# Mamba stage: convolution taps loaded by overlapping transfers, the scan's last columns kept by ScalarE, the convolution carry set earlier

## The chip, the cores and the metric

One NeuronCore of a Trainium2 chip runs the whole program. The metric is the device time of one execution in microseconds. The kernel before takes 4458.61 us (median of three runs, 4454.52 to 4467.43). The engines are TensorE (PE in the rows), VectorE (DVE), ScalarE (ACT), GpSimd (POOL) and SyncE (SP), which here only issues transfers. 16 DMA engines carry the transfers.

## The reference, cut to what matters

The network works on 16 images of 24 channels and 56 x 56 pixels. Four mixing layers (window attention, Mamba, four-way scan, row LSTM) alternate with quantised feed-forward layers. The change touches the Mamba layer alone. For a batch of images it computes:

```
x, gate   = 3x3 depthwise convolution of in_proj(normed)       # "taps": nine shifted copies of normed
xm, z     = in_proj2(x);  xm = silu(conv1d over 3 pixels(xm))   # needs the last 2 pixels of the part before: the carry
dt, B, C  = projections of xm;  dt = softplus(dt)
h[d,n]    = exp(dt*A[d,n]) * h[d,n] + dt*xm*B[n]                # a scan over the 3136 pixels, 48 channels x 16 states
y         = sum_n h[d,n]*C[n] + xm*D;  y = y * silu(z);  out = out_proj(...) * silu(gate)
```

## The kernel before, in words

The Mamba stage is `mamba_phase`, code written out for each engine in its own order, with semaphores between them. The image is cut into 7 stages of 8 rows (448 pixels). A *pair* (item `m`) is two images in one stage: 8 pairs in a stage, 56 in all. The scan works in *steps* `t` (336, 48 in a stage): two of the 16 states for 8 channels of all 16 images, so 128 lanes by 448 pixels. Eight steps are a pass (8 channels, all states), six passes a stage.

Each engine runs one loop over `j` from -11 to 66, in six slots `k`, with `t = 6j + k`. In iteration `j` the front work of pair `j+11` is done (project the taps, SiLU), the inner work of pair `j+10`, the rest of pair `j+9`, six scan steps, and the output work of pair `j-10`. So there are eleven iterations without scan steps, 45 with front work and scan steps, 11 with scan steps but no front work, and a tail.

- SP issues all transfers in order on one queue. In an iteration: the taps of pair `j+12` (`load_taps`, L1113, slot 0, two buffers), the store of B and C of pair `j+9` (L1143, `dram_bc<-mam_bcs`, 2 x 32 rows of 448), two stores each of dt, xm and z (L1121, 6 x 8 rows of 448 each), the store of the gate (L1138, `dram_gs<-mam_gs`, 128 rows); from pair 0 on also loads of dt and xm for a pass (`mam_ft`), of z (`mam_zy`) and the store of y; from `j` = 9 on loads of y and the gate (`mam_yt`, `mam_gt`) and stores of the result. In each stage four times two loads of B and C into 128 lanes (L1167, `mam_bs`, `mam_cs`, 896 KB each), the last of them behind the taps of an iteration.
- Taps: for each image of a pair nine transfers of 24 channels x 464 pixels (1856 bytes a row), one for each tap of the 3x3 window.
- DVE: two `drive` multiplications (L1500) and two scans (L1513) a step; every second step `save` (L1523) copies the last column of four rows of `h` into `kept`, where the next stage's scans start. `h` holds four steps.
- ACT: two `decay` exponentials a step (L1417), two steps ahead; then, in slots 3 to 5, SiLU and the logarithms of the front and inner work.
- POOL: `weigh` (L1570) each step; `carry` (L1578, L1580), which copies the two last pixels between parts of an image and stands in slot 1 of the iteration in which PE convolves, behind `series`; `clip` and `series`.
- PE: projections, `convolve` (L1257, waits for `carried`), and the sum over states (L1301).

Of the kernel before, what the change touches and what calls it, by code (L numbers as in the profile page):

```python
# [13 lines left out]
ACT = mybir.ActivationFunctionType  # L14
# [4 lines left out]
C = 24  # L19
# [8 lines left out]
PAD = SIDE + 2  # L28
PADDED = PAD * PAD + 4
# [5 lines left out]
def reached(eng, sem, value):  # L35

    if isinstance(value, int) and value <= 0:
        return
    eng.wait_ge(sem, value)  # L39
# [928 lines left out]
STATES = 16  # L968
# [17 lines left out]
def mamba_phase(nc, w, x, normed, mixed):  # L986
# [4 lines left out]
    with ExitStack() as ctx:  # L991
# [90 lines left out]
        def item(i):  # L1082
            return i if 0 <= i < ITEMS else None
# [7 lines left out]
        with nc.Block() as block:  # L1091
            @block.sync
            def _(sp):
# [11 lines left out]
                def load_taps(m):  # L1105
                    s, q = divmod(m, DUOS)
                    reached(sp, front_b, m - 1)
                    for i in range(2):
                        for tap in range(TAPS_5 + TAPS_4):
                            at = (8 * s + tap // 3) * PAD + tap % 3  # L1110
                            tile, row = ((taps_5, tap) if tap < TAPS_5
                                         else (taps_4, tap - TAPS_5))
                            sp.dma_start(tile[m % 2][i][C * row:C * row + C, :],  # L1113
                                         normed[2 * q + i, :, at:at + TAP_N]
                                         ).then_inc(taps_in[m % 2], 16)

                def keep_rows(dram, tile, m, sem):
# [115 lines left out]
            def _(pe):  # L1233
# [7 lines left out]
                def project(m, i):  # L1241

                    if i == 0:
                        pe.wait_ge(taps_in[m % 2], 288 * (m // 2 + 1))
                    ps = (ps_a, ps_b)[i]
                    for part, (tile, weights) in enumerate(((taps_5, win_5), (taps_4, win_4))):
                        rows = tile[m % 2][i][:].rearrange("c (r q) -> c r q", q=PAD)
                        mm = pe.matmul(ps[:, 0:MT], weights[:, i, :], rows[:, :, 0:SIDE],  # L1248
                                       start=(part == 0), stop=(part == 1))
                    mm.then_inc((front_a, front_b)[i], 1)  # L1250
# [84 lines left out]
            def _(act):  # L1335
# [74 lines left out]
                def decay(t):  # L1410
# [4 lines left out]
                    for i in range(2):  # L1415
                        at = p % DB * STATES + 2 * pair + i
                        act.activation(a[t % 3][:, i, :], ft[p % 2][:, 0, :], ACT.Exp,  # L1417
                                       scale=a_neg[:, at:at + 1]).then_inc(decays, 1)

                for j in range(FIRST, LAST):  # L1420
                    front, inner, r = item(j + LEAD), item(j + LEAD - 1), item(j - LAG)
                    for k in range(6):
                        t = 6 * j + k + 2
                        if 0 <= t < STEPS:
                            decay(t)
                        if k == 2 and item(j - LAG - 1) is not None:
                            take_result(j - LAG - 1)
                        if k == 3 and (front is not None or inner is not None):
                            load_silu(nc)
                            if front is not None:  # L1430
                                gate_image(front, 0)
                                gate_image(front, 1)
                            if inner is not None:
                                activate_inner(inner)
                                activate_z(inner)
                            load_exp_and_ln(nc)
                        if k == 4 and inner is not None:
                            step_logs(inner)
                        if k == 5 and inner is not None:
                            copy_bc(inner)  # L1440
                        if k == 5 and r is not None:
                            copy_inner(r)
                        if k == 5 and inner is not None:
                            quadratic(inner)

            @block.vector
            def _(dve):
# [55 lines left out]
                def scan(t, i):  # L1503
                    p, pair = divmod(t, 8)
                    n = 2 * t + i
                    at = p % DB * STATES + 2 * pair + i
                    dve.wait_ge(driven, n + 1)
                    if i == 0:
                        reached(dve, weighed, t - 3)
                        if t % 2 == 0:  # L1510
                            reached(dve, saved, (t - 48) // 2 + 1)
                    dve.wait_ge(decays, n + 1)
                    dve.tensor_tensor_scan(h[:, n % 8, :], a[t % 3][:, i, :], dbx[:, i, 0:MT],  # L1513
                                           kept[:, at:at + 1], ALU.mult, ALU.add
                                           ).then_inc(scanned, 1)

                def save(t):

                    p, pair = divmod(t, 8)
                    at = p % DB * STATES + 2 * pair - 2  # L1520
                    row = (2 * t - 2) % 8
                    dve.wait_ge(scanned, 2 * t + 2)
                    dve.tensor_copy(kept[:, at:at + 4], h[:, row:row + 4, MT - 1]  # L1523
                                    ).then_inc(saved, 1)

                def times_z(p):
                    dve.wait_ge(accumulated, 8 * (p + 1))
# [12 lines left out]
                for j in range(FIRST, LAST):  # L1540
                    previous = item(j + LEAD - 2)
                    for k in range(6):
                        t = 6 * j + k
                        if 0 <= t < STEPS:
                            if t % 8 == 0:
                                make_u(t // 8)
                            drive(t, 0)
                            drive(t, 1)
                        if t % 2 == 0 and 0 < t <= STEPS:
                            save(t - 1)  # L1550
                        if t % 8 == 3 and 0 <= t // 8 - 1 < PASSES:
                            times_z(t // 8 - 1)
                        if k == 2 and previous is not None:
                            step_size(previous)
                        if 0 <= t < STEPS:
                            scan(t, 0)
                            scan(t, 1)

            @block.gpsimd
            def _(pool):  # L1560
# [36 lines left out]
                    pool.tensor_tensor(yi[:], yi[:], gt[r % 2][:], ALU.mult).then_inc(gated, 1)  # L1597

                for j in range(FIRST, LAST):
                    inner, previous = item(j + LEAD - 1), item(j + LEAD - 2)  # L1600
                    for k in range(6):
                        t = 6 * j + k
                        if 0 <= t < STEPS:
                            weigh(t)
                        if k == 0 and previous is not None:
                            series(previous)
                        if k == 0 and item(j - LAG - 1) is not None:
                            times_gate(j - LAG - 1)
                        if k == 1 and inner is not None:
                            carry(inner)  # L1610
                        if k == 4 and inner is not None:
                            clip(inner)

# [639 lines left out]
```

## Time and profile before

| | us |
|---|---|
| median of three runs | 4458.61 |
| the profiled execution's own time | 4458.26 |
| its span | 4456.6 |
| Mamba stage within it, from its first load (1022.70) to the next layer's first load (2656.51) | 1634 |

Busy time in the whole span: PE 3640.5 us (82%), DVE 2888.3 (65%), ACT 2692.4 (60%), POOL 1600.1 (36%). A time in the trace counts from the span's start. The busy share of DMA is a mean over the 16 DMA engines: 0.13 is two of sixteen engines busy. For DMA a packet is one row of data or one small write of a semaphore.

### The profile page before, as it was taken

What the parts mean: (1) busy time and instruction counts of PE and PEld (TensorE: products, weight loads), DVE (VectorE), ACT (ScalarE), POOL (GpSimd) and SP (SyncE); (2) the same over time, 40 slices, a digit from 0 to 9 for tenths busy, and PEclk for the clock granted to TensorE, in tenths of its full rate; (3) what the DMA queues carried; (4) which work ended last, traced back from release to release, by engine and by line L of the source; (5) the groups of instructions that cost most, each with busy time, mean ns of one, the idle gap of its engine ahead of it and who ended that gap; (6) DMA issues with size and microseconds to landing.
All of it is one profiled execution on the core that took longest, in us unless ns stands there. A gap on an engine that the chain in (4) does not pass through costs nothing. (4 is left out here: it accounts for less than half of the span.)

```text
span 4456.6 us, 73149 instructions
## 1 busy us (share of the span) xinstructions
PE 3640.5 (82%) x20680; PEld 2121.9 (48%) x20680; DVE 2888.3 (65%) x4570; ACT 2692.4 (60%) x4664; POOL 1600.1 (36%) x1447
## 2 busy tenths in 40 slices
PE   4899999785677888888876658689999786799956
PEld 2788888442233333333332214344444332799932
DVE  2666666671289989898999937566666665111146
ACT  4555555695666767676765328677777576233346
POOL 0333333101366767676766630045555400000000
PEclk9999999897889989999999979899999988899979
DMA  3000000123536364646544122100000022100012
GB/s 92 19 15 14 14 14 14 35 57 99 152 102 162 116 177 116 172 125 166 152 135 129 52 69 50 39 16 15 15 15 15 9 53 71 34 11 11 11 44 53
DMA packets 203144, 296.59 MB, mean 67 GB/s; under 512 B 68686, under 2 KB 188670, under 8 KB 202242
## 3 DMA queue, kind: packets, MB, share of 16 engines
q1 hardware_dynamic: 193798, 285.57, 24.4%
q10 hardware_dynamic: 9216, 9.65, 0.9%
q8 instruction: 37, 0.61, 0.1%
q14 instruction: 93, 0.76, 0.1%
HBM read 193.01 MB, written 102.03 MB: 66 GB/s over the span
## 5 line engine op out<-in xcount | busy, mean ns | idle before, releaser
L1570 POOL TENSOR_TENSOR mam_hc<-mam_h,mam_cs 128x896 f32<-128x896 f32 x336 | 712.5, 2126 | 333.4 <-DVE mam_h L1513 317.3
L1301 PE MATMUL mam_ps_y<-mam_hc,mam_ident 128*128 128x448 f32 x1344 | 628.4, 595 | 211.0 <-POOL mam_hc L1570 211.0
L1513 DVE TENSOR_TENSOR_SCAN mam_h<-mam_a,mam_kept,mam_dbx 128x448 f32<-128x448 f32 x672 | 729.3, 1123 | 1.2 <-ACT mam_a L1417 1.2
L1417 ACT ACTIVATE mam_a<-mam_ft,mam_a_neg 128x448 f32<-128x448 f32 x672 | 402.1, 656 | 242.4 <-DVE mam_h L1513 241.8
L1944 POOL TENSOR_TENSOR scan_ch<-scan_h,scan_cs 128x392 f32<-128x392 f32 x256 | 344.2, 1360 | 560.8 <-DVE scan_h L1910 560.8
L1301 PEld LDWEIGHTS mam_ps_y<-mam_hc,mam_ident 128*128 128x128 f32 x1344 | 261.3, 204 | 550.0 <-POOL mam_hc L1570 330.7
L1500 DVE TENSOR_TENSOR mam_dbx<-mam_ps_u,mam_bs 128x448 f32<-128x448 f32 x672 | 381.8, 611 | 92.5 <-DMA mam_cs<-dram_bc 91.1
L756 POOL TENSOR_TENSOR att_prob<-att_prob,att_share 128x588 f32<-128x588 f32 x128 | 151.9, 1186 | 452.1 <-DVE att_share L941 452.1
L1910 DVE TENSOR_TENSOR_SCAN scan_h<-scan_turned_in,scan_start 128x392 f32<-128x392 f32 x192 | 256.6, 1356 | 25.6 <-ACT scan_turned_in L1829 24.2
L1784 PE MATMUL scan_ps_merged<-scan_ch,scan_w_merge 128*128 128x392 f32 x512 | 230.6, 532 | 47.8 <-POOL scan_ch L1944 46.0
L2034 PE MATMUL lstm_ps<-lstm_hs,lstm_w_h 128*128 (+1 forms) x1344 | 264.9, 352 | 0.0
L2034 PEld LDWEIGHTS lstm_ps<-lstm_hs,lstm_w_h 128*128 128x128 f32 x1344 | 253.1, 188 | 3.0
L2084 DVE TENSOR_TENSOR lstm_kept<-lstm_gates,lstm_cell 128x224 f32<-128x224 f32 x56 | 22.0, 392 | 347.3 <-ACT lstm_gates L2055 347.3
L408 PE MATMUL f_xc_ff<-all_x,f_centre 128*128 (+1 forms) x256 | 128.3, 585 | 145.2 <-DVE all_x L298 145.2
L2025 PE MATMUL lstm_ps<-lstm_xs,lstm_w_x 128*128 (+1 forms) x896 | 181.4, 354 | 57.7 <-DMA lstm_xs<-in_rl_ones 57.7
L1784 PE MATMUL scan_ps_gate<-scan_ch,scan_w_merge 128*128 128x392 f32 x512 | 211.0, 494 | 0.0
L369 ACT ACTIVATE f_h<-f_hid 96x784 f16<-96x784 f32 x256 | 207.0, 811 | 0.0
L876 ACT ACTIVATE att_pt<-att_ps_t 128x512 f32<-128x512 f32 x128 | 76.4, 597 | 210.0 <-PE att_ps_t L817 210.0
L857 ACT ACTIVATE att_keys<-att_ps_keys 24x392 f32<-24x392 f32 x384 | 186.7, 486 | 22.8 <-PE att_ps_keys L785 19.8
L1772 PE MATMUL scan_ps_in<-scan_xin,scan_w_in 128*128 128x392 f32 x512 | 184.8, 505 | 17.6 <-DVE scan_ub L1919 15.4
L2025 PEld LDWEIGHTS lstm_ps<-lstm_xs,lstm_w_x 128*128 128x128 f32 x896 | 169.6, 189 | 61.1 <-issue 58.9
L1248 PE MATMUL mam_ps_a<-mam_taps,mam_win 120*128 120x448 f32 x224 | 121.9, 675 | 93.6 <-ACT mam_yi L1403 84.4
(215 smaller groups left out, 7984.1 us busy)
## 6 DMA issues: line engine op xcount, KB each, us to landing
mam_taps<-normed SPq DMA_DIRECT2D x1008, 43.5 KB
mam_bs<-dram_bc SPq DMA_DIRECT2D x28, 896.0 KB, 11.6
mam_cs<-dram_bc SPq DMA_DIRECT2D x28, 896.0 KB, 16.9
mam_ft<-dram_steps SPq DMA_DIRECT2D x42, 448.0 KB, 5.1
normed<-f_staged SPq DMA_DIRECT2D x384, 38.1 KB
f_mixed<-mixed SPq DMA_DIRECT2D x384, 36.8 KB
dram_gs<-mam_gs SPq DMA_DIRECT2D x56, 224.0 KB, 2.7
mam_gt<-dram_gs SPq DMA_DIRECT2D x56, 224.0 KB
```

What stands on the lines that cost most here:

```text
L369: act.activation(h16[:, 2 * a:2 * a + 2, :], hid[a][0:HID, :, 0:N], ACT.Copy).then_inc(ff["hidden16"], 1)
L857: o = act.activation(keys[p][0:C, :, h * T:(h + 1) * T], ps_keys[32 * h:32 * h + C, 0:N].rearrange("c (w t) -> c w t", w=WINS), ACT.Copy)
L1301: mm = pe.matmul(ps_y[p % 2][:, 0:MT], ident[:], hc[t % 2][:, i, :], start=False, stop=(t % 8 == 7 and i == 1))
L1417: act.activation(a[t % 3][:, i, :], ft[p % 2][:, 0, :], ACT.Exp, scale=a_neg[:, at:at + 1]).then_inc(decays, 1)
L1500: dve.tensor_tensor(dbx[:, i, 0:MT], ps_u[:, 0:MT], bs[:, 2 * pair + i, :], ALU.mult).then_inc(driven, 1)
L1513: dve.tensor_tensor_scan(h[:, n % 8, :], a[t % 3][:, i, :], dbx[:, i, 0:MT], kept[:, at:at + 1], ALU.mult, ALU.add).then_inc(scanned, 1)
L1570: pool.tensor_tensor(hc[t % 2][:], h[:, row:row + 2, :], cs[:, 2 * pair:2 * pair + 2, :], ALU.mult).then_inc(weighed, 1)
L1784: mm = pe.matmul(ps[:, 0:N], w_merge[:, a, n, :], ch[p][:, n, :], start=(n == 0), stop=(n == DIRS - 1))
L1910: dve.tensor_tensor_scan(out, a, v, start[p][:, n:n + 1], ALU.mult, ALU.add).then_inc(scanned, 1)
L1944: pool.tensor_tensor(out, hd, in_order(cs, 1 - half, d, t, p), ALU.mult).then_inc(weighed, 1)
L2025: pe.matmul(ps[p][:, q, 0:W], w_x[:, tap, q, :], xs[:, :, bass.ds(y + 1, 1), tap:tap + SIDE].rearrange("c j o q -> c j (o q)"), start=(tap ...
L2034: mm = pe.matmul(ps[p][:, q, 0:W], w_h[:, tap, q, :], hs[:, :, bass.ds(y, 1), tap:tap + SIDE].rearrange("c j o q -> c j (o q)"), start=Fal ...
```

## The change

`load_taps` issues four transfers an image in place of nine. One transfer takes the `n` taps of one image row that differ in their column shift alone: its source overlaps itself (outermost dimension `n` with a stride of one element, then 24 channels, then 464 pixels), its target is `24n` rows of the tile. `n` is 3, 2, 1 and 3. `save` (in the diff as it stands on ACT; the function on DVE goes) moves from DVE to ACT, as an activation behind `decay`, and a scan now waits for the save of three steps before. `carry` of a pair stands in slot 4 of the iteration in which its front work is done, ahead of `clip`.

```diff
-                        for tap in range(TAPS_5 + TAPS_4):
-                            at = (8 * s + tap // 3) * PAD + tap % 3
-                            tile, row = ((taps_5, tap) if tap < TAPS_5
-                                         else (taps_4, tap - TAPS_5))
-                            sp.dma_start(tile[m % 2][i][C * row:C * row + C, :],
-                                         normed[2 * q + i, :, at:at + TAP_N]
+                        for tile, row, dy, dx, n in ((taps_5, 0, 0, 0, 3), (taps_5, 3, 1, 0, 2),
+                                                     (taps_4, 0, 1, 2, 1), (taps_4, 1, 2, 0, 3)):
+                            shifted = bass.AP(
+                                tensor=normed.tensor,
+                                offset=(2 * q + i) * C * PADDED + (8 * s + dy) * PAD + dx,
+                                ap=[[1, n], [PADDED, C], [1, TAP_N]])
+                            sp.dma_start(tile[m % 2][i][C * row:C * (row + n), :], shifted
                                          ).then_inc(taps_in[m % 2], 16)
...
-                        pe.wait_ge(taps_in[m % 2], 288 * (m // 2 + 1))
+                        pe.wait_ge(taps_in[m % 2], 128 * (m // 2 + 1))
...
+                def save(t):
+
+                    p, pair = divmod(t, 8)
+                    at = p % DB * STATES + 2 * pair - 2
+                    row = (2 * t - 2) % 8
+                    act.wait_ge(scanned, 2 * t + 2)
+                    act.activation(kept[:, at:at + 4], h[:, row:row + 4, MT - 1], ACT.Copy
+                                   ).then_inc(saved, 1)
...
                         if 0 <= t < STEPS:
                             decay(t)
+                        if t % 2 == 0 and 0 <= t - 3 < STEPS:
+                            save(t - 3)
...
-                            reached(dve, saved, (t - 48) // 2 + 1)
+                            reached(dve, saved, t // 2 - 1)
...
-                        if t % 2 == 0 and 0 < t <= STEPS:
-                            save(t - 1)
...
-                        if k == 1 and inner is not None:
-                            carry(inner)
+                        if k == 4 and front is not None:
+                            carry(front)
                         if k == 4 and inner is not None:
                             clip(inner)
```

On SP, an iteration before the first scan step reads like this in the kernel before:

```order
L1113 DMA mam_taps<-normed 24x464 x18
L1143 DMA dram_bc<-mam_bcs 2x32x448
L1121 DMA dram_steps<-mam_dt 6x8x448 x2
L1121 DMA dram_steps<-mam_xm 6x8x448 x2
L1121 DMA dram_zs<-mam_zs 6x8x448 x2
```

and so in the changed one (the shapes of the taps are those of the target):

```order
L1115 DMA mam_taps<-normed 72x1x464
L1115 DMA mam_taps<-normed 48x1x464
L1115 DMA mam_taps<-normed 24x464
L1115 DMA mam_taps<-normed 72x1x464 x2
L1115 DMA mam_taps<-normed 48x1x464
L1115 DMA mam_taps<-normed 24x464
L1115 DMA mam_taps<-normed 72x1x464
L1144 DMA dram_bc<-mam_bcs 2x32x448
L1122 DMA dram_steps<-mam_dt 6x8x448 x2
L1122 DMA dram_steps<-mam_xm 6x8x448 x2
L1122 DMA dram_zs<-mam_zs 6x8x448 x2
```

Eight transfers stand where 18 stood, with the same 432 rows of data in all; the rest of the iteration keeps its place.

On POOL, the start of the Mamba stage in the kernel before (L1578 and L1580 are the carry, L1585 `clip`, L1590 and L1592 `series`):

```order
L1578 COPY mam_xg<-mam_tails 128x2
L1580 COPY mam_tails<-mam_xg 128x2
L1585 ISA
L1585 TENSOR_SCALAR mam_es<-mam_ex 128x448
L1590 TENSOR_TENSOR mam_es<-mam_quad,mam_es 128x448
L1592 TENSOR_TENSOR mam_es<-mam_es,mam_rv 128x448
L1578 COPY mam_xg<-mam_tails 128x2
L1580 COPY mam_tails<-mam_xg 128x2
```

and in the changed one:

```order
L1579 COPY mam_xg<-mam_tails 128x2
L1581 COPY mam_tails<-mam_xg 128x2
L1579 COPY mam_xg<-mam_tails 128x2
L1581 COPY mam_tails<-mam_xg 128x2
L1586 ISA
L1586 TENSOR_SCALAR mam_es<-mam_ex 128x448
L1591 TENSOR_TENSOR mam_es<-mam_quad,mam_es 128x448
L1593 TENSOR_TENSOR mam_es<-mam_es,mam_rv 128x448
L1579 COPY mam_xg<-mam_tails 128x2
```

The carry of a pair has moved ahead of `clip` and `series` of the pair before it.

## Rows read from the trace of the kernel before

**Rows 1.** Busy us (instructions) of each engine by stretch; then PEclk, DMA share, GB/s.
```profile
1030.00:1190.00 160.00, 106.09 (x206) 44.18 (x207) 9.63 (x23) 102.15 (x157) 38.98 (x47) 0.80 0.42 112
...
1600.00:1650.00 50.00, 40.16 (x91) 17.57 (x90) 39.55 (x52) 32.17 (x54) 30.37 (x21) 0.90 0.84 227
1650.00:1800.00 150.00, 130.87 (x304) 57.17 (x303) 146.01 (x183) 111.11 (x184) 110.67 (x76) 0.93 0.43 122
...
2346.00:2600.00 254.00, 161.83 (x343) 62.51 (x342) 253.59 (x316) 103.57 (x175) 159.76 (x85) 0.93 0.30 83
```

**Rows 2.** Waits of DVE, 1000 to 2450 us: for whom, us in total, times, longest.
```profile
DVE mam_dbx L1500 <- DMA mam_cs<-dram_bc: 91.1, 16, 16.9
...
DVE mam_h L1513 <- ACT mam_a L1417: 1.2, 2, 0.8
```

**Rows 3.** Instructions of L1523: duration min/median/max, first and last start.
```profile
L1523 DVE COPY mam_kept<-mam_h x168: 148/992/1943, 1211.8 to 2600.1; 128x4 f32<-128x4 f32 x168
```

**Rows 4.** Group by line, 1200 to 2400 us: busy us, mean ns, idle before.
```profile
L1523 DVE COPY mam_kept<-mam_h 128x4 f32<-128x4 f32 x141 | 107.2, 760 | 0.0
```

**Rows 5.** Group by line, 2346 to 2600 us.
```profile
L1523 DVE COPY mam_kept<-mam_h 128x4 f32<-128x4 f32 x33 | 35.4, 1073 | 0.0
```

**Rows 6.** Instructions of L1138: issue ns min/median/max, first and last start.
```profile
L1138 SPq DMA_DIRECT2D dram_gs<-mam_gs x56: 349/460/3872, 1046.2 to 2346.4; - x56
```

**Rows 7.** Timeline of SP, 1170 to 1260 us.
```profile
1180.70 0.46 SPq L1138 DMA_DIRECT2D dram_gs<-mam_gs  x1
```

**Rows 8.** Groups by line on ACT, 1046 to 1190 us.
```profile
L1361 ACT ACTIVATE mam_xm<-mam_ps_c,mam_conv_b 128x448 f32<-128x448 f32 x9 | 5.7, 635 | 36.5 <-PE mam_ps_c L1257 36.5
...
L1389 ACT ACTIVATE mam_bcs<-mam_ps_c 64x448 f32<-64x448 f32 x9 | 4.7, 521 | 0.0
```

**Rows 9.** Timeline of SP before the scans: start, us, what it issues, count.
```profile
1071.13 7.94 SPq L1113 DMA_DIRECT2D mam_taps<-normed  x18
1079.12 0.58 SPq L1143 DMA_DIRECT2D dram_bc<-mam_bcs  x1
1079.76 1.47 SPq L1121 DMA_DIRECT2D dram_steps<-mam_dt  x2
1083.37 1.42 SPq L1121 DMA_DIRECT2D dram_steps<-mam_xm  x2
1084.84 1.42 SPq L1121 DMA_DIRECT2D dram_zs<-mam_zs  x2
1086.30 0.46 SPq L1138 DMA_DIRECT2D dram_gs<-mam_gs  x1
```

**Rows 10.** Short stretches, columns as in rows 1.
```profile
1071.00:1072.00 1.00, 1.00 (x4) 0.41 (x3) 0.00 (x0) 1.00 (x3) 0.00 (x0) 1.00 0.59 222
1080.30:1081.00 0.70, 0.70 (x2) 0.29 (x2) 0.00 (x0) 0.00 (x0) 0.00 (x0) 0.50 0.13 20
1081.00:1083.00 2.00, 2.00 (x5) 0.84 (x4) 0.00 (x0) 0.29 (x1) 0.00 (x0) 0.76 0.25 60
1085.20:1086.40 1.20, 1.20 (x4) 0.68 (x4) 0.00 (x0) 1.19 (x4) 0.00 (x0) 1.00 0.35 117
1087.00:1088.00 1.00, 1.00 (x5) 0.42 (x3) 0.00 (x0) 0.97 (x2) 0.97 (x1) 1.00 0.73 231
1200.00:1220.00 20.00, 7.50 (x13) 3.04 (x14) 15.07 (x20) 6.58 (x10) 10.39 (x8) 0.71 0.92 239
```

**Rows 11.** DMA, 1075 to 1079 us: packets, queue share, what was issued.
```profile
DMA packets 384, 0.47 MB, mean 117 GB/s; under 512 B 133, under 2 KB 384, under 8 KB 384
...
q1 hardware_dynamic: 384, 0.47, 48.0%
...
mam_taps<-normed SPq DMA_DIRECT2D x10, 43.5 KB
```

**Rows 12.** DMA, 1020.5 to 2660 us: packets, queue share.
```profile
DMA packets 113459, 213.08 MB, mean 130 GB/s; under 512 B 22145, under 2 KB 100732, under 8 KB 113371
...
q1 hardware_dynamic: 113371, 212.16, 47.2%
```

More of the change, by code:

```diff
@@ L1515, in scan @@
                                            ).then_inc(scanned, 1)
[L1517 to L1524, printed above, removed]
                 def times_z(p):
@@ L1599, in _ @@
                 for j in range(FIRST, LAST):
-                    inner, previous = item(j + LEAD - 1), item(j + LEAD - 2)
+                    front, inner = item(j + LEAD), item(j + LEAD - 1)
+                    previous = item(j + LEAD - 2)
                     for k in range(6):
```

## The prediction

> **What bounds the kernel now.** I read the busy times by stretch first [rows 1]. Of the 1634 us of the Mamba stage only the part with scan steps, from about 1200 us on, is DVE's: 146 of 150 us between two stage borders, 253.6 of 254 us once the front work is over. Before the scans no engine is full (ACT 102, PE 106 of 160 us), and at a stage border (1600 to 1650 us) DVE drops to 39.6 of 50 us while the DMA share is 0.84. The waits of DVE say for what: 91.1 us in 16 waits for the loads of B and C, 1.2 us for ACT [rows 2]. So there are three regimes: eleven iterations in a loop of engines, SP and DMA; 45 iterations of DVE with DMA-bound borders; 11 iterations of DVE alone.
>
> DVE carries a cost that looks like nothing: `save` copies 4 numbers a lane and takes 148 ns at best but 992 ns in the median and up to 1943 ns [rows 3]; 760 ns in the mean with front work beside it [rows 4], 1073 ns later [rows 5]. Next the pace ahead of the scans: the gate stores, one an iteration, start at 1046.2 us first [rows 6] and at 1180.70 us nine iterations later [rows 7], so an iteration takes (1180.7 - 1046.2) / 9 = 14.9 us. In it ACT waits 36.5 us in nine for PE's convolution, 4.1 us each [rows 8]; the convolution waits for the carry. SP issues 18 taps in 7.94 us, and all its transfers take 7.94 + 0.58 + 1.47 + 1.42 + 1.42 + 0.46 = 13.3 us [rows 9], so it is nearly full.
>
> **How wide a transfer is.** The taps' new source has 3 or 2 as its outermost count, so I looked at what narrow ones do. In 1080.30 to 1081.00 us the store of B and C (2 x 32 rows), issued at 1079.12, is alone: the DMA share is 0.13, two of sixteen engines [rows 9, 10]. In 1085.20 to 1086.40, with stores of 6 x 8 rows issued one behind the other, it is 0.35, about six [rows 9, 10]. The taps now: 384 packets, 133 of them small (semaphores), hence 251 rows, about one semaphore write for two rows: 24 rows on 12 engines [rows 11]. And all packets of that kind in the stage, 22145 [rows 12], are near what widths of 12 for 1008 taps (12,096), 6 for 448 stores and loads of 6 x 8 rows (2688), 2 for 56 (112), 12 for 112 results (1344) and 16 for 294 transfers of 128 rows (4704) give: 20,944, the rest being small rows of weights. The width follows the outermost counts of source and target: 2, 6, 12 and 16 are the greatest common divisors up to 16. For 3 against 72 that is 3, for 2 against 48 it is 2; the single tap stays at 12. In 1081 to 1083 us, where that store and two 6-wide ones overlap, the share is 0.25, four engines and not the eight of separate sets [rows 10]: I take the narrow ones to share the same first engines.
>
> The Trainium skill, "DMA: Bandwidth & Descriptors", section on why a DMA increments its semaphore by 16, states this rule (the largest number up to 16 that divides the slowest dimension of both patterns, on the lowest-numbered engines); by that rule the new taps run on engines 0 to 2, and without it one would count on 12 engines, as in rival A. It speaks against this change; the trace agrees for widths of 2, 6 and 12.
>
> **Load of the first DMA engine.** In rows of data. Taps now: 18 x 2 = 36 a pair. After: four transfers of 72 rows on 3 engines are 4 x 24, two of 48 on 2 are 2 x 24, two of 24 on 12 are 2 x 2: 148. Beside them in an iteration: six stores of 48 rows on 6 engines, 6 x 8 = 48; 64 rows on 2 engines, 32; the gate's 128 on 16, 8: 88. Sum 124 before, 236 after.
>
> Price of a row of 1792 or 1856 bytes: at the fastest the trace shows, 222 GB/s at a share of 0.59 is 23.5 GB/s an engine, 79 ns; 231 at 0.73 is 19.8 GB/s, 94 ns [rows 10]. The mean over every packet of the stage is 0.472 x 16 x 1639.5 us / 113,371 = 109 ns [rows 12]. I take 90 ns, between the two full stretches, since a queue of 24 rows on an engine is nearer to these; the ends are 79 and 109.
>
> **The change part by part.**
>
> 1. Ahead of the scans. The first engine needs 236 x 0.090 = 21.2 us an iteration, against 14.9 us now. Two pairs of taps are in flight, so its queue does not run dry, and the loop takes its pace: 9 x (21.2 - 14.9) = +57 us. The ends: 18.6 us gives +34, 25.7 us gives +97. The first pair takes 148 x 0.090 = 13.3 us on the engine in place of the 7.94 us of its issue: +6 us (+4 and +8).
>
> 2. Carry set sooner, eight issues for eighteen. Both gains lie here: ACT's 4.1 us an iteration goes, and SP's 13.3 us becomes at most 13.3 - 7.94 + 6 x 0.74 + 2 x 0.44 = 10.7 us (a three-dimensional one taken at a dt store's 1.47 / 2 us, a plain one at 7.94 / 18 = 0.44). What is late next is not ACT (14.9 - 4.1 = 10.8 us) but the DMA engine, so they are worth 0. On POOL nothing queues: the carry waits for the SiLU of slot 3, `clip` behind it for a later ACT instruction.
>
> 3. Iterations with front work and scans. From 1180.7 to the last gate store at 2346.4 us [rows 6, 7] there are 46 in 1165.7 us. First engine, after: 236 rows plus the pass loads and stores (0.75 of 8 double rows, 8 and 8: 24), 260 x 0.090 = 23.4 us; in 36 of them also y, gate and result, 16 + 8 + 4 = 28 rows, 2.5 us; six sets of B and C, 64 packets of 7168 bytes each, at 305 ns (23.5 GB/s) to 441 ns (239 GB/s at 0.92, rows 10), taken as 375: 24 us. Sum 46 x 23.4 + 36 x 2.5 + 6 x 24 = 1076 + 90 + 144 = 1310 us, +145. At 79 ns and 305: 1139, -27. At 109 and 441: 1582, +416. Here the 135 saves that leave DVE (some 103 us) buy nothing: DVE waits for DMA in their place, at the borders above all.
>
> 4. Iterations without front work. No taps; DVE is full. 33 saves of 1073 ns go: -35 us [rows 1, 5].
>
> 5. `save` on ACT. The trace has no ACT instruction of four columns; the nearest is 521 ns for a 64 x 448 copy [rows 8]. Between 0 and 0.52 us, three an iteration; ACT is busy 111 of 150 us [rows 1], so 1.6 us of its 6 idle ones hide it. If that cover were gone it would cost up to 46 x 1.6 = 74 us. The new wait of a scan is for a save issued right behind a decay that runs two steps ahead, and behind the waiting scan stand only DVE's own scan and drive: 0, by the 1.2 us that DVE ever waited for ACT.
>
> Sum: +57 + 6 + 145 - 35 = +173 us against the profiled execution's 4458.3 us, which is the median's 4458.6 within 0.4: **4631 us**, 3.9% slower.
>
> **Rivals.**
>
> A. *The narrow transfers do not bind* (the source's outermost 3 is not what splits it, or the engines differ from one transfer to the next). Then the change does what it says: 9 x -4.1 = -37 us ahead of the scans, -103 and -35 us of saves, +12 at the borders, where DVE arrives earlier by three saves of 0.8 us at five of them and the loads do not: 4295 us. For it: the taps before never held anyone up, and the queue would carry fewer issues. Against it: the widths of 2 and 6 in rows 10. Chance 0.08.
>
> B. *The first engine keeps up*: long queues read at the fastest rate, 79 ns. +34 + 4 - 27 - 35 = -24: 4434 us, faster by 0.5%. It decides below 80 ns a row; at 85 ns the sum is already +97. For it: four-fold longer runs on an engine. Against it: 94 ns at the higher of the full stretches, and DVE and DMA waiting for each other at the borders adds something always. Chance 0.14, a third of it within 0.3%.
>
> C. *Rows as dear as the stage's mean*, 109 ns: +97 + 8 + 416 - 35 = +486: 4944 us. For it: the 109 ns. Against it: that mean holds the big rows of B and C. Chance 0.12.
>
> **How the numbers follow.** The forecast has 0.66. A measurement of this kernel tells about 0.3% (13 us) from no change. Faster: A and two thirds of B, 0.08 + 0.09 = 0.17. Same: 0.05. Slower: 0.66 + 0.12 = 0.78. The likeliest case's own range, 83 to 100 ns a row, is 4520 to 4790. The range that should hold the time 8 times in 10 reaches from 4430, which takes in B, to 4850, which takes in half the way to C.
>
> **What would show it.** The small packets of the stage fall by about 9850 (12,096 become 4 x 56 x 3 + 2 x 56 x 2 + 2 x 56 x 12 = 2240). Gate stores ahead of the scans stand about 21 us apart, with a DMA share no higher than now though every iteration waits for DMA. PE or ACT waits for taps, or for the stores of dt, xm and B and C behind them. DVE's waits for the loads of B and C grow from 91 us to some 250, at each border. In 2346 to 2600 us's counterpart, steps take 3.2 us without a copy. I am wrong if gate stores come every 11 us (rival A), or if they come every 21 us and the scans all the same run at DVE's pace.

## The result, and the profile after

The changed kernel takes **4529.74 us** (median of four runs, 4528.43 to 4534.48) against 4457.66 (four runs): 1.016 times the time of before [1.0142, 1.0177], 72 us slower. The forecast was 4631, 173 us slower: direction and range hold, the size does not. The profiled execution took 4530.17 us, its span 4528.5.

First, three groups of instructions of the kernel after: the gate stores, the scans and the saves, with duration in ns (min/median/max) and first and last start.

```profile
L1139 SPq DMA_DIRECT2D dram_gs<-mam_gs x56: 364/460/5037, 1050.1 to 2443.8; - x56
...
L1525 DVE TENSOR_TENSOR_SCAN mam_h<-mam_a,mam_kept,mam_dbx x672: 1109/1124/1149, 1238.2 to 2670.3; 128x448 f32<-128x448 f32 x168
...
L1427 ACT ACTIVATE mam_kept<-mam_h x168: 190/192/208, 1244.7 to 2671.5; 128x4 f32<-128x4 f32 x168
```

And the scans of the kernel before:

```profile
L1513 DVE TENSOR_TENSOR_SCAN mam_h<-mam_a,mam_kept,mam_dbx x672: 1109/1124/1147, 1204.0 to 2598.9; 128x448 f32<-128x448 f32 x168
```

The first scan starts 34 us later, the last one 71 us later, which is the whole difference. The marks of [rows 6] and [rows 7] split it as the prediction did:

| stretch | before | after | difference | forecast |
|---|---|---|---|---|
| to the first gate store | 1046.2 | 1050.1 | +4 | +6 |
| nine iterations ahead of the scans | 134.5 | 157.9 | +23 | +57 |
| 46 iterations, to the last gate store | 1165.7 | 1235.8 | +70 | +145 |
| from there to the last scan | 252.5 | 226.5 | -26 | -35 |
| sum | | | +71 | +173 |

The gate stores ahead of the scans in the timeline of SP, kernel after, answer to [rows 7, 9] (start, us, what is issued; other issues between them are left out):

```profile
1096.08 0.46 SPq L1139 DMA_DIRECT2D dram_gs<-mam_gs  x1
1113.19 0.45 SPq L1139 DMA_DIRECT2D dram_gs<-mam_gs  x1
1130.59 0.46 SPq L1139 DMA_DIRECT2D dram_gs<-mam_gs  x1
1148.13 0.46 SPq L1139 DMA_DIRECT2D dram_gs<-mam_gs  x1
1165.24 0.45 SPq L1139 DMA_DIRECT2D dram_gs<-mam_gs  x1
```

They stand 17.3 us apart, (1165.24 - 1096.08) / 4; 21.2 were forecast. Spread over the 236 rows that the prediction counts for the first DMA engine, that is 73 ns a row. DMA in 1020.5 to 2731.5 us of the kernel after, the stretch of [rows 12] moved with the stage's end:

```profile
DMA packets 103551, 212.88 MB, mean 124 GB/s; under 512 B 12316, under 2 KB 90828, under 8 KB 103468
```

The small packets fall by 22145 - 12316 = 9829, where 9850 were forecast: the count fits loads on three, two and twelve engines. Busy time by stretch, kernel after, columns as in [rows 1]:

```profile
1030.00:1212.00 182.00, 109.49 (x206) 46.35 (x206) 9.61 (x23) 100.48 (x154) 35.98 (x47) 0.78 0.27 94
1212.00:1270.00 58.00, 29.51 (x53) 11.88 (x54) 20.69 (x25) 28.27 (x48) 18.01 (x14) 0.71 0.71 180
...
2444.00:2666.00 222.00, 150.80 (x333) 59.18 (x332) 215.10 (x276) 106.09 (x206) 156.18 (x82) 0.95 0.35 94
```

Ahead of the scans PE waits for the taps, 55.7 us in 10 waits from 1046 to 1212 us (before 2.4 us in 2, 1046 to 1190 us), while the mean DMA share *falls*, from 0.42 to 0.27: a mean over sixteen engines does not show one that is full. In 1212 to 1270 us DVE works 21 of 58 us; 26 of these lie ahead of the first scan, and from there on it works 19.6 of 31.8. What it waits for, 1000 to 2735 us, kernel after (us in total, times, longest):

```profile
DVE mam_dt L1540 <- POOL mam_es L1593: 169.1, 9, 38.7
DVE mam_dbx L1512 <- DMA mam_cs<-dram_bc: 155.5, 14, 28.1
DVE mam_dt L1540 <- issue: 75.0, 35, 2.8
...
DVE mam_dbx L1512 <- issue: 27.6, 5, 7.6
DVE mam_h L1525 <- ACT mam_kept L1427: 12.2, 11, 2.3
```

The first row is the stretch ahead of the scans, where DVE has nothing else. The loads of B and C cost 155.5 + 27.6 us against 91.1 [rows 2]; of these 28.1 and 16.9 are one wait ahead of the first scan. The 27.6 are five waits of `drive` at stage borders for which the profile names no releaser. 183 us is less than the 250 that the prediction gave as a sign. New is the third row, `step_size` (L1540), 75 us in 35 short waits (13.5 in 8 before). Its cause is seen in the timeline of the kernel after, 1776 to 1801 us (idle time before an instruction in brackets):

```profile
1778.00 1.33 POOL L1586 TENSOR_SCALAR mam_es<-mam_ex 128x448 f32<-128x448 f32 x1 [3.11 <-ACT mam_ex L1380]
...
1779.41 4.14 POOL L1571 TENSOR_TENSOR mam_hc<-mam_h,mam_cs 128x896 f32<-128x896 f32 x2
...
1783.49 1.15 POOL L1591 TENSOR_TENSOR mam_es<-mam_quad,mam_es 128x448 f32<-128x448 f32 x1
...
1784.72 1.13 POOL L1593 TENSOR_TENSOR mam_es<-mam_es,mam_rv 128x448 f32<-128x448 f32 x1
...
1785.94 1.48 DVE L1540 SCALAR_TENSOR_TENSOR mam_dt<-mam_ln,mam_consts,mam_es 128x448 f32<-128x448 f32 x1 [2.45 <-issue]
```

POOL's `series` ends at 1784.72 + 1.13 = 1785.85 and `step_size` starts 0.09 us later: DVE, three copies an iteration lighter, arrives before POOL is done and waits there. DVE's account from the start of the first scan to the end of the last:

| DVE, us | before (1204.0 to 2600.0) | after (1238.2 to 2671.4) | difference |
|---|---|---|---|
| busy | 1304.0 | 1187.8 | -116 |
| waits at `drive` for B and C | 74.3 | 127.4 + 27.6 | +81 |
| waits at `step_size` | 13.5 | 75.0 | +61.5 |
| scans waiting for ACT | 1.2 | 12.2 + 1.6 | +12.6 |
| sum | | | +39 |
| measured | 1396.0 | 1433.2 | +37 |

The 168 copies of 814 ns in the mean are 137 us, but DVE's busy time falls by 116: the records of its instructions overlap in part, by 72 us in the scans' stretch of before and by 57 after.

### The profile page after: what moved, and what is told of

Read it like the earlier page. It is cut to its first block and busy times, and to the rows that moved or that the text cites. A ratio compares the mean times of both kernels' runs of the same rounds, so it can differ in the third digit from the quotient of the medians.

```text
span 4528.5 us, 72611 instructions
## 1 busy us (share of the span) xinstructions
PE 3652.1 (81%) x20680; PEld 2129.2 (47%) x20680; DVE 2769.1 (61%) x4402; ACT 2711.9 (60%) x4832; POOL 1596.2 (35%) x1447
## 5 line engine op out<-in xcount | busy, mean ns | idle before, releaser
L1525 DVE TENSOR_TENSOR_SCAN mam_h<-mam_a,mam_kept,mam_dbx 128x448 f32<-128x448 f32 x672 | 729.7, 1125 | 13.9 <-ACT mam_kept L1427 12.2
L1512 DVE TENSOR_TENSOR mam_dbx<-mam_ps_u,mam_bs 128x448 f32<-128x448 f32 x672 | 382.3, 613 | 184.4 <-DMA mam_cs<-dram_bc 155.5
L1249 PE MATMUL mam_ps_a<-mam_taps,mam_win 120*128 120x448 f32 x224 | 141.5, 770 | 195.9 <-ACT mam_yi L1404 107.9
L1540 DVE SCALAR_TENSOR_TENSOR mam_dt<-mam_ln,mam_consts,mam_es 128x448 f32<-128x448 f32 x56 | 81.2, 1451 | 244.3 <-POOL mam_es L1593 169.1
## 6 DMA issues: line engine op xcount, KB each, us to landing
mam_cs<-dram_bc SPq DMA_DIRECT2D x28, 896.0 KB, 19.6
```

What stands on the lines that cost most here:

```text
L1512: dve.tensor_tensor(dbx[:, i, 0:MT], ps_u[:, 0:MT], bs[:, 2 * pair + i, :], ALU.mult).then_inc(driven, 1)
```

## The experiments

Each ratio is to runs of the kernel before on the same chip, with its 95% interval.

**The three parts alone.** `e1_taps_only`: the kernel before with the new `load_taps` and its wait.

```diff
 # kernel before
-   nine sp.dma_start(... normed[2 * q + i, :, at:at + TAP_N])
+   four sp.dma_start(... ap=[[1, n], [PADDED, C], [1, TAP_N]])
-   pe.wait_ge(taps_in[m % 2], 288 * (m // 2 + 1))
+   pe.wait_ge(taps_in[m % 2], 128 * (m // 2 + 1))
```

> The kernel before with the eight overlapping loads alone. Theory 1 (the overlapping loads run on 3 and 2 DMA engines, and the first of these sets the pace ahead of the scans and at the stage borders): gate stores 17 to 18 us apart ahead of the scans (before 14.9), waits of DVE for B and C near 150 us (before 91), all saves still on DVE: 4540 to 4600 us. Theory 2 (the loss comes from save on ACT or from the new place of the carry): 4430 to 4460 us.

Measured: 4557.73 us, ratio 1.0209 [1.0192, 1.0226], **+97 us**. Gate stores are 17.2 us apart, the first scan starts at 1239.2. So the loads alone cost more than the whole change loses.

`e2_save_only`: the kernel before with the copy on ACT.

```diff
 # kernel before, ACT, slot k
+                        if t % 2 == 0 and 0 <= t - 3 < STEPS:
+                            save(t - 3)
 # DVE
-                            reached(dve, saved, (t - 48) // 2 + 1)
+                            reached(dve, saved, t // 2 - 1)
...
-                        if t % 2 == 0 and 0 < t <= STEPS:
-                            save(t - 1)
```

> The kernel before with save on ACT alone. Theory 1: 119 us less busy time on DVE, of which some 50 come back where step_size, no longer delayed by a save, waits for POOL's series, and 15 at the stage borders: 4380 to 4410 us. Theory 2 (save on ACT gives everything back in waits of the scans for ACT): 4450 to 4480 us.

Measured: 4427.69 us, ratio 0.992 [0.9903, 0.9936], **-33 us**, where more was expected: DVE's busy time falls by 111 us, and the stretch from the first to the last scan by 31 (1394.9 to 1364.4). The gate stores tell where: the 46 iterations with front work, which hold 135 of the 168 copies, are 6 us shorter (1159.4 for 1165.7), the stretch behind them 24 us. Waits of DVE, `e2_save_only`, 1000 to 2735 us:

```profile
DVE mam_dbx L1511 <- DMA mam_cs<-dram_bc: 98.3, 15, 16.0
DVE mam_dt L1539 <- issue: 76.4, 36, 3.0
...
DVE mam_h L1524 <- ACT mam_kept L1426: 10.2, 12, 1.7
```

`step_size` takes 63 us back with the taps untouched, B and C 8 and the scans' waits for ACT 11: that give-back belongs to `save`, not to the loads.

`e3_carry_only`: the kernel before with `carry` in slot 4 of the earlier iteration.

```diff
 # kernel before, POOL
-                        if k == 1 and inner is not None:
-                            carry(inner)
+                        if k == 4 and front is not None:
+                            carry(front)
```

> The kernel before with the earlier carry alone. Theory 1: PE's 5 us of waiting for the carry goes, SP's 13.3 us of issuing an iteration become the pace ahead of the scans: nine to ten times 1.5 us, 4440 to 4450 us. Theory 2 (SP was not near its limit): ACT's 10.8 us pace, 4415 to 4425 us. If the new place costs time in the scans (POOL waits for the SiLU): above 4458 us.

Measured: 4446.75 us, ratio 0.9962 [0.9948, 0.9977], **-14 us**. Gate stores come 13.6 us apart. The parts sum to 97 - 33 - 14 = +50; together they are +72. The first scan of after is as late as that of `e1_taps_only` (1238.2 and 1239.2), so behind the narrow loads the carry's gain is gone, as step 2 had it.

**Is it the width?** `e4_wide_all`: the same four overlapping loads an image with the channel outermost in place of the tap; the weights' rows follow the new order (not shown here).

```diff
 # kernel after
-                                ap=[[1, n], [PADDED, C], [1, TAP_N]])
+                                ap=[[PADDED, C], [1, n], [1, TAP_N]])
```

> The changed kernel, but the channel is the outermost dimension of each overlapping load (and the weights' rows are ordered by channel to match): the same eight loads, bytes and rows, on 12 engines. Theory 1: gate stores 11 to 13 us apart ahead of the scans, waits of DVE for B and C back to 90 to 110 us, 4350 to 4400 us. Theory 2 (reading the same rows three times, or three-dimensional loads as such, cost the time): 4510 to 4540 us, as the changed kernel.

Measured: 4387.61 us, ratio 0.9837 [0.9814, 0.9861]: 142 us faster than after with the same bytes, rows and instructions. Gate stores of `e4_wide_all`, timeline of SP:

```profile
1078.99 0.46 SPq L1139 DMA_DIRECT2D dram_gs<-mam_gs  x1
1090.77 0.46 SPq L1139 DMA_DIRECT2D dram_gs<-mam_gs  x1
1102.54 0.45 SPq L1139 DMA_DIRECT2D dram_gs<-mam_gs  x1
```

11.8 us apart. Its waits for B and C are 84.5 us, and `step_size` still waits 76.8. The order of two dimensions is the whole of the loss. This kernel also shows what rival A stood for: the change with loads that do not bind gains 1.6%, 70 us and not rival A's 163. Its first scan starts 27 us sooner than before's (rival A: 37), and from there to the last scan it gains 42 us (rival A: 126).

**What does a row cost on the first engine?** Two kernels change its number of rows in an iteration. `e5_half_wide` gives the channel-outermost form, with the weights' rows to match, to the two-tap loads alone: 236 - 2 x 24 + 2 x 4 = 196 rows.

```diff
 # kernel after
+                            rows = [[1, n], [PADDED, C]] if n != 2 else [[PADDED, C], [1, n]]
-                                ap=[[1, n], [PADDED, C], [1, TAP_N]])
+                                ap=rows + [[1, TAP_N]])
```

> The changed kernel with the channel outermost in the loads of two taps alone (48 rows on 12 engines in place of 2; the loads of three taps stay on 3). Theory 1: the first DMA engine has 196 rows an iteration in place of 236; at the 73 ns a row that 17.3 us for 236 rows give, gate stores ahead of the scans stand 14.3 us apart, and of the 64 us of longer waits for B and C a fourth to a half goes: 4455 to 4495 us. Theory 2 (the number of engines of the widest narrow load counts, not the rows on the first engine): pace 17.3 us and 4530 us as in the changed kernel.

Measured: 4450.72 us, ratio 0.9983 [0.9971, 0.9995], a little below the range expected. Gate stores of `e5_half_wide`:

```profile
1082.25 0.46 SPq L1140 DMA_DIRECT2D dram_gs<-mam_gs  x1
1096.38 0.46 SPq L1140 DMA_DIRECT2D dram_gs<-mam_gs  x1
1110.63 0.46 SPq L1140 DMA_DIRECT2D dram_gs<-mam_gs  x1
1125.23 0.46 SPq L1140 DMA_DIRECT2D dram_gs<-mam_gs  x1
1139.53 0.46 SPq L1140 DMA_DIRECT2D dram_gs<-mam_gs  x1
```

(1139.53 - 1082.25) / 4 = 14.3 us, or 73 ns a row.

`e9_after_bc16` leaves the taps narrow and widens another transfer: the store of B and C, 32 rows on the first engine, goes to a buffer laid out so that it has 64 rows outermost, by the same count 4 on each of 16 engines: 208 rows. The buffer's declaration and its loads change with it (not shown here).

```diff
 # kernel after
-                    sp.dma_start(bc_d[2 * q:2 * q + 2, s], bcs[:]).then_inc(bc_out, 16)
+                    sp.dma_start(bc_d[s, 2 * q:2 * q + 2].rearrange("i r n -> (i r) n"), bcs[:]
+                                 ).then_inc(bc_out, 16)
...
```

> The changed kernel with the layout of the stored B and C turned in DRAM, so that their store has 64 rows outermost on both sides and runs on 16 engines in place of 2. The narrow taps stay. Theory 1 (all narrow transfers share the first engines, and the first one's rows set the pace): 236 - 28 = 208 rows, at 73 ns 15.3 us between gate stores ahead of the scans, 4480 to 4505 us. Theory 2 (narrow transfers of different shapes use different engines, or the length of a taps load alone counts): pace 17.3 us, 4520 to 4535 us.

Measured: 4492.81 us, ratio 1.008 [1.0061, 1.0099], and in the timeline of SP of `e9_after_bc16`:

```profile
1089.95 0.46 SPq L1139 DMA_DIRECT2D dram_gs<-mam_gs  x1
...
1166.28 0.46 SPq L1139 DMA_DIRECT2D dram_gs<-mam_gs  x1
```

Five iterations lie between these two: 15.3 us each, 73 ns a row. Three kernels with 236, 208 and 196 rows on the first engine give 17.3, 15.3 and 14.3 us. That the rows of B and C's store count in the same sum as the taps' is what shared first engines give; on separate sets of engines the pace would have stayed at 17.3.

**Where beside the scans is it lost?** Two complementary kernels. Pairs 3 and 4 of every eight are loaded in the iterations in which the loads of B and C are issued (12 of these 14 pairs; the first two are loaded ahead of any load of B and C). `e11_border_single` loads these (14 of 56 pairs) by the 18 single transfers of before, the others narrow; `e12_border_narrow` the other way round.

```diff
 # kernel after (e12: "not in")
+        def alone(m):
+            return m % 8 in (3, 4)
...
+                        if alone(m):
+                            groups = [... nine of n = 1 ...]
-                        pe.wait_ge(taps_in[m % 2], 128 * (m // 2 + 1))
+                        pe.wait_ge(taps_in[m % 2], sum(288 if alone(x) else 128
+                                                       for x in range(m % 2, m + 1, 2)))
```

> The kernel after, but the taps of the two iterations in each stage in which the loads of B and C are issued (pairs 3 and 4 of every eight, 14 of 56 pairs) come by the 18 single transfers of the kernel before (12 engines); the other 42 pairs keep the narrow ones. Same results. Base for the share: before with save (-33) and carry (-14) alone would be about 4414 us, so the narrow taps cost 4530 - 4414 = 116 us in it. Of these some 40 us lie ahead of the scans in either theory, 5 of which go with two iterations. Theory 1 (at a stage border the narrow taps stand ahead of the loads of B and C in the first engines' queues, and that is all they cost beside scans): 4460 to 4480 us, DVE's waits for B and C (183 us with those called issue) down to 100 to 130. Theory 2 (every narrow iteration costs its share, 1.6 to 2 us): 4495 to 4510 us, waits for B and C 150 to 180.

Measured: 4452.99 us, ratio 0.9992 [0.9981, 1.0002]: by ratios 75 us (0.0168 x 4458) faster than after, from a quarter of the pairs; more than Theory 1 asked (its lower end is 4460). Scans of `e11_border_single`:

```profile
L1532 DVE TENSOR_TENSOR_SCAN mam_h<-mam_a,mam_kept,mam_dbx x672: 1108/1125/1148, 1225.5 to 2603.6; 128x448 f32<-128x448 f32 x168
```

and its waits of DVE:

```profile
DVE mam_dbx L1519 <- DMA mam_cs<-dram_bc: 113.1, 18, 21.5
DVE mam_dt L1547 <- issue: 74.7, 35, 3.0
```

> The complement: narrow taps for pairs 3 and 4 of every eight alone, the 18 single transfers for the other 42. Same results. Theory 1: 4414 + 60 to 75 = 4470 to 4490 us, DVE's waits for B and C 140 to 175 us, though only a quarter of the pairs is loaded narrow; gate stores ahead of the scans 13.6 to 15 us apart but for two iterations. Theory 2: a quarter of the cost beside scans, 4414 + 5 + 20 = 4430 to 4445 us, waits for B and C about 115 us.

Measured: 4495.34 us, ratio 1.0086 [1.007, 1.0103], just above Theory 1's range and 50 us outside Theory 2's. Scans and waits of `e12_border_narrow`:

```profile
L1532 DVE TENSOR_TENSOR_SCAN mam_h<-mam_a,mam_kept,mam_dbx x672: 1108/1125/1148, 1203.2 to 2635.1; 128x448 f32<-128x448 f32 x168
```

```profile
DVE mam_dbx L1519 <- DMA mam_cs<-dram_bc: 158.8, 15, 28.6
...
DVE mam_dbx L1519 <- issue: 22.3, 5, 6.3
```

From first to last scan: `e2_save_only` 1364.4 us, `e11_border_single` 1378.1, `e12_border_narrow` 1431.9, after 1432.1. So the two narrow pairs at each border make the scans' stretch as long as all eight do. The 14 us of `e11_border_single` are at most what the other six add: its profiled execution, 4466.69 us, is the slowest of its ten and 13.7 above their median.

What happens at a border is in SP's timeline. Kernel after, first border:

```profile
1239.43 14.98 SPq L1115 DMA_DIRECT2D mam_taps<-normed  x8
1254.45 1.45 SPq L1144 DMA_DIRECT2D dram_bc<-mam_bcs  x1
1255.95 2.20 SPq L1154 DMA_DIRECT2D mam_ft<-dram_steps  x1
1258.20 0.59 SPq L1168 DMA_DIRECT2D mam_bs<-dram_bc  x1
```

The eight taps, 5.4 us of issue in mid-stage (5.44 at 1776.60), take 14.98, and the last loads of B and C start 18.8 us behind the taps' start. With singles there (before, `e11_border_single`) it is 13.8 us, with narrow ones (`e12_border_narrow`) 18.9. The whole set of loads stands further apart still. The third border, the first and the last load of B in the set with the taps between them, kernel before:

```profile
1591.49 0.60 SPq L1167 DMA_DIRECT2D mam_bs<-dram_bc  x1
...
1611.47 10.97 SPq L1113 DMA_DIRECT2D mam_taps<-normed  x18
...
1624.07 0.57 SPq L1167 DMA_DIRECT2D mam_bs<-dram_bc  x1
```

and kernel after:

```profile
1641.96 2.05 SPq L1168 DMA_DIRECT2D mam_bs<-dram_bc  x1
...
1670.23 14.64 SPq L1115 DMA_DIRECT2D mam_taps<-normed  x8
...
1688.65 0.59 SPq L1168 DMA_DIRECT2D mam_bs<-dram_bc  x1
```

From the first to the last it is 32.6 us before and 46.7 after. In the mean of the six borders that have taps it is 32.6 us before, 32.7 in `e2_save_only` and `e11_border_single`, 45.2 after, 45.3 in `e12_border_narrow`: 12.5 us more with narrow taps there. Once issued, the last load of C, for which DVE waits longest (17.4 us at this border), lands as soon as before: 16.5 us before and 16.8 after in the mean. The first two of the four loads of C do land later, at the third border 18.0 us after issue for 11.7 before, and 24.8 for 17.7. But what DVE waits for longest at a border is a load that SP issues late, not one that moves slowly.

**Where does `step_size` wait?** `e6_after_slot3` moves it on DVE one slot back, behind two more scans.

```diff
 # kernel after, DVE
-                        if k == 2 and previous is not None:
+                        if k == 3 and previous is not None:
                             step_size(previous)
```

> The changed kernel with step_size one slot later on DVE. Theory 1a (DVE's 75 us of waiting at step_size are a wait for POOL's series, which is late since the saves have left DVE; the first DMA engine does not bound the iterations between borders): 61 to 75 us less waiting there, part of it given back at borders and at ACT, 4470 to 4505 us. Theory 1b (the first DMA engine paces every iteration with front work, as forecast): no change, 4525 to 4535 us.

Measured: 4506.92 us, ratio 1.0101 [1.0085, 1.0118], just above the range expected. Waits of DVE in `e6_after_slot3`:

```profile
DVE mam_dbx L1512 <- DMA mam_cs<-dram_bc: 151.7, 14, 27.8
...
DVE mam_dbx L1512 <- issue: 39.0, 5, 10.1
DVE mam_h L1525 <- ACT mam_kept L1427: 31.4, 38, 2.2
```

The 75 us are gone and the time falls by 23 to 26: part comes back at the borders (39.0 for 27.6), part as a new wait of the scans for ACT's copies (31.4 for 12.2), and DVE's busy time in the scans' stretch is 17 us longer (1204.5 for 1187.8), most of it in `step_size` itself (88.7 for 75.1).

**The best version.** `e7_wide_slot3` is `e4_wide_all` with that slot. `e8_wide_slot3_late` also issues the taps in slot 1, behind loads of B and C and of the gate:

```diff
 # e7_wide_slot3, SP
-                        if k == 0 and item(j + LEAD + 1) is not None:
-                            load_taps(j + LEAD + 1)
...
+                        if k == 1 and item(j + LEAD + 1) is not None:
+                            load_taps(j + LEAD + 1)
```

> The wide loads with step_size one slot later on DVE. If the wait at step_size is a wait of place alone: 4387 less 50 to 70 us, 4320 to 4340 us. If another chain (ACT's, at 75% busy) sets an iteration of some 23 us just behind: 4375 to 4390 us, with longer waits of the scans for ACT.

> As the kernel before this one, and the taps are issued in slot 1 behind the last load of B and C and the loads of y, no longer in slot 0 ahead of them. If what DVE waits for at a border is a load issued late behind the taps: some 8 to 10 us less at each of five borders, 40 to 50 us faster than e7. If it is the DMA engines' throughput at the border, or if the taps now come late: no gain.

Measured: 4359.59 us, 0.9773 [0.9756, 0.979], and 4351.55 us, 0.9746 [0.9729, 0.9762]. Both miss: the first lies between its two ranges, the second is 8 us faster than the first where 40 to 50 or nothing was expected. In `e7_wide_slot3` the scans wait for the copies:

```profile
DVE mam_dbx L1512 <- DMA mam_cs<-dram_bc: 96.4, 17, 20.1
...
DVE mam_h L1525 <- ACT mam_kept L1427: 36.1, 49, 2.4
```

In `e8_wide_slot3_late` B and C fall to 81.3 and the copies rise to 46.7: with wide loads the order of issue is worth little. The order was not tried with narrow ones. `e10_best_bc16` adds the wide store of B and C of `e9_after_bc16`:

> The wide taps, step_size one slot later, the taps issued behind the last load of B and C, and the store of B and C on 16 engines. If the first engine still binds at the borders: 10 to 25 us below e8 (4327 to 4342 us). If the 16 engines' common throughput binds there: within 5 us of e8's 4352 us.

Measured: **4341.93 us**, ratio 0.9732 [0.9714, 0.9751], the fastest here: 2.7% below the kernel before and 4.2% below after (0.9732 / 1.016). Against `e8_wide_slot3_late` it is 9.6 us less, by the ratios 6 us, and the intervals of the two overlap: this does not decide between its two expectations.

## Why the prediction was right or wrong

*Which engines.* Right. The width was read from the share of DMA and the count of small packets before, and their fall was forecast within 21 of 9829. `e4_wide_all` shows that the order of the dimensions alone turns a gain into the loss. The rule in the Trainium skill, "DMA: Bandwidth & Descriptors", section on why a DMA increments its semaphore by 16, says the same of the width, and the small packets agree with it. In `e4_wide_all`, with channels outermost, small packets are 15294 (stage end aligned), 2978 above after; twelve engines for the 336 loads would give 224 x 9 + 112 x 10 = 3136.

*Step 1, ahead of the scans.* Right mechanism; its size hangs on the row's price, taken as 90 ns with 79 and 109 as ends. It is 73 ns in three kernels, outside these bounds. The bounds came from two stretches of 1 us of mixed traffic [rows 10] and from the mean of the whole stage [rows 12]; none showed one engine with a long queue of such rows. (The Trainium skill, "DMA: Bandwidth & Descriptors", Specifications, gives about 27 GiB/s an engine: an estimate by it is 64 ns for a row of 1856 bytes; the runs lie above it, and the end of 79 ns should have been lower.) With 73 ns the term is 9 x (17.2 - 14.9) = +21; measured +23.

*Step 2, the carry.* Right: nothing behind narrow loads, though it is worth 14 us alone.

*Step 3 failed.* It said that the first DMA engine paces the 46 iterations with scans, 1310 us of rows, +145; measured are 1235.8 us, +70. With 73 ns a row, and 285 ns for a packet of 7168 bytes at the same rate (an estimate), its own sum gives 46 x 260 x 0.073 + 36 x 28 x 0.073 + 6 x 64 x 0.285 = 1056 us, less than the 1165.7 of before: the engine would never bind, and the sum would foretell a gain. Yet 70 us were lost. Between borders the first engine does not set the pace: gate stores come some 23.3 to 24.3 us apart in mid-stage in the kernels before, after and `e4_wide_all` alike, and an iteration of after (23.4 us, `step_size` to `step_size`, 1762.51 to 1785.94) has 288 x 73 ns = 21 us of rows. That the step's 260 rows at 90 ns also give 23.4 us is chance. The loss lies at the borders, as `e11_border_single` and `e12_border_narrow` show: two narrow pairs at each make the whole of it, 68 us of scan stretch (1431.9 - 1364.4), 11 us for each of six borders. What the timelines add is how: SP's issue of the set of loads of B and C takes 12.5 us longer, and the last of them, for which DVE waits longest, is that much later and no slower. A throughput sum over a long stretch cannot see this.

Why SP's issue stretches is not shown. The likely reason is that the first engines' queues are full: two iterations have 2 x 112 x 73 ns = 16 us more rows for the first of them. That is arithmetic, not a measurement, and it holds in proportion only in part: of the 68 us of scan stretch, `e9_after_bc16` with 84 of the 112 rows loses 50 (1414.5 - 1364.4), where 51 would be in proportion, but `e5_half_wide` with 72 of them 27 (1391.0 - 1364.4) and not 43. Narrow taps issued behind the loads of B and C would test it and were not tried.

*"135 saves buy nothing."* Nearly right in amount, by another cause: in `e2_save_only`, without narrow loads, the 46 iterations gain 6 us from them. Of the 111 us by which DVE's busy time falls there, 63 come back at `step_size`, 11 at the scans and 8 at B and C; of the 31 that are kept, 24 lie behind the last gate store. The prediction took the time saved to go to DMA; the first taker was a wait for POOL of which before shows 13.5 us, and which the prediction did not name.

*Step 4* was -35 and is -26: DVE was taken as full there, and 6.7 us of it are waits at `step_size` (3.6) and for B and C (3.1). *Step 5*: the copy costs ACT 192 ns, in its range of 0 to 520; the new wait, put at 0 from 1.2 us of waiting for ACT, is 12 us, and 31 to 47 once `step_size` no longer waits.

*Rival B* (4434) had the row's price nearly right and the result wrong: a row below 80 ns was said to decide for a gain, and it does not, since the border is no matter of mean rate. Its own argument against itself, that DVE and DMA waiting for each other at the borders always adds something, was the answer. Two errors of opposite sign stand in the forecast's size: the price too high, the late issue at the borders left out. That the measured time lies inside the range is luck in part: with 73 ns throughout, the sum is 21 + 3 - 110 - 35 = -121, 4337 us, below the range. Rival C (4944) is refuted. Rival A (4295) is excluded by the packet count; the kernel in which its condition holds, `e4_wide_all`, takes 4388 us, 92 more than it said, since the copies on ACT gave back most of what they freed.

## What to carry to other kernels

An overlapping load that gathers shifted copies saves issues, but the dimension that stands outermost decides how many DMA engines carry it; put the long one (channels) there and check the count of small packets. When a transfer is narrow, add up the rows of the first engine for the pace of a loop, and apart from that look at which load is issued behind it on the same queue where an engine waits for that load, and when it is issued: a mean busy share shows neither. Before crediting work taken off a full engine, look for its next wait in each iteration, however small it is now.

## What the runs showed of the hardware

- Rows of 1792 and 1856 bytes in a long queue on one DMA engine cost 73 ns each (24.5 to 25.4 GB/s), as the pace of three kernels divided by their rows on the first engine gives it; the two full stretches of before that the prediction used gave 79 and 94 ns.
- Copying the last column of four rows, 128 x 4, takes ACT 190 to 208 ns and took DVE 148 to 1943, 814 in the mean, beside POOL's work. The Trainium skill, "ScalarE: Activation LUTs", section on what ACT_TABLE_LOAD costs, has 186 ns + 0.833 ns an element for an activation without pointer operands, 189 ns for four; the runs agree, and the range of 0 to 520 could have been a number. Why DVE's varies was not tested.
- The issue of eight taps by SP stretches from 5.4 to 14.98 us at a border, and that of 18 single ones from 7.94 [rows 9] to 12.04 (before, first border); what SP waits for within it is not shown. The last load of C, 896 KB, issued behind them, lands 15.8 to 17.6 us after its issue in either kernel.
